# One mask product for both query tiles, the geodesic difference in halves, clips of two banks, and a new instruction order

## What is computed

```python
cos = jnp.einsum('bhsd,bhtd->bhst', q, k)            # q, k of length 1
g_dist = jnp.arccos(jnp.clip(cos, -1.0 + EPS, 1.0 - EPS))
attn_score = (1.0 + g_dist) ** (-3.2)
```

## Time and profile before

| | |
|---|---|
| median of 3 runs | 2499.11 us |
| the profiled execution's own time | 2502.13 us |
| its span, first to last instruction | 2500.8 us |
| TensorE busy with products | 1993.4 us, 10866 instructions |
| VectorE busy | 1930.0 us, 3005 |
| ScalarE busy | 1833.5 us, 2759 |
| GpSimd busy | 525.0 us, 206 |
| mean granted TensorE clock | 0.842 of full speed |

### The profile page before, as it was taken

How to read it: one execution, slowest core, us unless ns; L and a number is a source line. 1 busy time by engine, 2 the same in 40 slices (tenths; PEclk the granted TensorE clock), 3 DMA queues, 4 the chain that set the end, 5 groups by cost and what they waited for, 6 DMA issues and landing times.

```text
span 2500.8 us, 32678 instructions
## 1 busy us (share of the span) xinstructions
PE 1993.4 (80%) x10866; PEld 1328.3 (53%) x10866; DVE 1930.0 (77%) x3005; ACT 1833.5 (73%) x2759; POOL 525.0 (21%) x206
## 2 busy tenths in 40 slices
PE   4777778888678878878787888878787878888867
PEld 2544546775345555655465555655455555655645
DVE  5788895545997889699867889699968889674554
ACT  3436868697669677887777787887678786978883
POOL 2413121022112121302212121302112211221220
PEclk8787878999887888888787989888687989776778
DMA  7631112432211110111001110111001010000000
GB/s 250 222 98 56 51 34 67 131 116 85 83 42 53 46 35 18 40 35 55 22 13 48 39 48 13 40 46 53 13 31 39 32 53 1 1 1 5 1 1 5
DMA packets 67527, 126.29 MB, mean 51 GB/s; under 512 B 8836, under 2 KB 40132, under 8 KB 67236
## 3 DMA queue, kind: packets, MB, share of 16 engines
q1 hardware_dynamic: 61808, 113.19, 13.9%
q0 software_dynamic: 2816, 7.21, 0.8%
q10 hardware_dynamic: 2740, 3.80, 0.4%
HBM read 111.33 MB, written 12.85 MB: 50 GB/s over the span
## 4 chain that ended last, share of the span: by engine, by line
PE 31%; DVE 30%; ACT 18%; issue 16%; DMA 2%; SPq 1%; POOL 1%; DVEq 0%; ACTq 0%; POOLq 0%
PE ps L763 6%; DVE hB L1434 5%; PE ps L984 4%; PE ps L942 4%; DVE hB L1428 3%; DVE hB L1440 2%; PE ps L1068 2%; ACT arena L1255 2%; ACT arena L1331 2%; PE ps L1043 2%; DVE arena L1506 2%; DVE n_c L1513 2%; ACT L758 2%; PE ps L1103 2%; DVE lss L1568 2%
## 5 line engine op out<-in xcount | busy, mean ns | idle before, releaser
L1726 POOL TENSOR_TENSOR arena<-arena 128x2048 f32<-128x2048 f32 x64 | 297.5, 4649 | 1188.9 <-ACT arena L1257 1188.8
L763 PE MATMUL ps<-w_ident,arena 128*128 128x128 f32 x1647 | 301.1, 319 | 123.6 <-ACT arena L1331 43.7
L942 PE MATMUL ps<-hB,w_ident 128*128 128x512 f32 x512 | 303.4, 725 | 75.3 <-DVE hB L1440 75.2
L763 PEld LDWEIGHTS ps<-w_ident,arena 128*128 128x128 f32 x1647 | 227.7, 166 | 234.1 <-issue 139.1
L1434 DVE TENSOR_TENSOR_SCAN hB<-dA,hB 128x1024 f32<-128x1024 f32 x128 | 324.6, 2539 | 9.1 <-ACT dA L1219 8.8
L1730 POOL TENSOR_TENSOR arena<-arena,rb 128x1024 f32<-128x1024 f32 x64 | 151.9, 2374 | 574.6 <-DVE rb L1566 574.6
L1219 ACT ACTIVATE dA<-dtv,w_A_log 128x510 f32<-128x510 f32 x256 | 168.8, 718 | 109.6 <-DVE hB L1434 108.6
L1043 PE MATMUL ps<-w_l_wqkv,arena 128*128 128x512 f32 x384 | 212.5, 677 | 33.7 <-DVE lss L1568 15.5
L1506 DVE TENSOR_SCALAR arena<-ps 128x512 f32<-128x512 f32 x256 | 163.8, 681 | 63.6 <-PE ps L984 62.8
L1331 ACT ACTIVATE arena<-ps,nmx 128x128 f32<-128x128 f32 (+1 forms) x512 | 158.9, 397 | 65.5 <-DVE nmx L1588 64.8
L942 PEld LDWEIGHTS ps<-hB,w_ident 128*128 128x128 f32 x512 | 106.3, 229 | 181.9 <-issue 116.2
(11 more groups left out here) (198 smaller groups left out, 4216.3 us busy)
## 6 DMA issues: line engine op xcount, KB each, us to landing
BC<-bc_d SPq DMA_DIRECT2D x128, 512.0 KB, 3.7
BC<-in_experts SPq DMA_DIRECT2D x31, 514.0 KB, 3.3
arena<-in_experts SPq DMA_DIRECT2D x15, 514.0 KB, 3.6
arena<-in_x SPq DMA_DIRECT2D x8, 256.0 KB, 5.8
xnT_d<-arena SPq DMA_DIRECT2D x8, 256.0 KB, 3.7
hB<-xnT_d SPq DMA_DIRECT2D x8, 256.0 KB, 2.6
x<-in_x SPq DMA_DIRECT2D x8, 256.0 KB, 2.9
out<-go SPq DMA_DIRECT2D x8, 256.0 KB, 2.3
```

Source lines behind the costliest of these rows:

```text
L763: return t.transpose(out_, in_, ident[0:k, 0:k])
L942: e = t.matmul(lb(), ident, hB[k % 2][:, j], start=q == 0 and j == 0, stop=q == NQ - 1 and j == NG - 1)
L1726: g.tensor_tensor(la[m % 2], la[m % 2], cl, ALU.subtract).then_inc(g_sub, 1)
```

## The change

- **Mask.** A `score` unit writes the mask of a head for both query tiles with one product of 320 columns (256 products in all instead of 512), and both mask products now stand ahead of all score products.
- **Difference.** `g_sub` becomes two GpSimd instructions of 128 by 1024, each for two heads. The clips of a half wait only for the same half of the block before; tanh and `f_tr`, whose tile shares memory with `cl`, wait for both halves.
- **Clips.** The two clips of a `g_score` unit become one over both banks (128 instructions of 128 by 1024). For this `choose` gives `g_score` two neighbouring banks.
- **Order.** `LATER`, `SWITCH` and the four constants have new values, `STREAM` adds an offset for some pairs of a kind of block (Mamba, geodesic, window layers), and three durations in `STAGES` differ (`g_score` VectorE 1.3 to 1.2, `g_sub` 4.6 to 2.4 a half, `score` TensorE 1.7 to 1.4). Every unit may change its place in the lists.

```diff
-SWITCH = 67.0
+SWITCH = 79.0
...
+STREAM = {("g", 5): -52, ("l", 0): -2, ("l", 2): -4, ("l", 6): 1, ("l", 7): -2, ("m", 1): -1, ("m", 2): -5, ("m", 4): -1,
+          ("m", 6): 17, ("m", 7): -10}
...
+def stream(unit):
+    u, n, b, k = unit
+    if u in [x for x, _ in LAYER]:
+        return "l", n // LAY
+    return ("-" if u == "m_weights" else u[0][0]), n
...
-        want[what] = time + LATER.get(what[0], 0.0)
+        want[what] = time + LATER.get(what[0], 0.0) + STREAM.get(stream(what), 0.0)
...
-EARLY, FIRST, SECOND, PERIOD = 49.0, 120.0, 105.0, 239.0
+EARLY, FIRST, SECOND, PERIOD = 120.0, 130.0, 80.0, 210.0
...
-        if unit[0] != "score":
+        if unit[0] not in ("score", "g_score"):
             return sorted(idle[0:count]) if len(idle) >= count else None
         pairs = [[z, z + 1] for z in range(7) if z in idle and z + 1 in idle]
...
+        def two_banks(unit):
+            z0, z1 = plan["banks"][unit]
+            return ps[:, z0:z1 + 1:z1 - z0]
...
+                    for z in range(2):
+                        t.matmul(lb(z)[:, 0:SC], ident_b[:], mask_b[:], start=True, stop=False)
                     for qt in range(2):
-                        for z in range(2):
-                            cols = slice(P, SC) if qt else slice(0, P)
-                            t.matmul(lb(z)[:, cols], ident_b[:], mask_b[:, cols], start=True, stop=False)
                         for z in range(2):
...
-                    a.wait_ge(g_sub, m + 1)
+                    a.wait_ge(g_sub, 2 * (m + 1))
...
                     if m:
-                        v.wait_ge(g_sub, m)
+                        v.wait_ge(g_sub, 2 * (m - 1) + k % 2 + 1)
                     v.wait_ge(p_gs, 2 * m + k % 2 + 1)
-                    for z in range(2):
-                        v.tensor_scalar(cl[:, 2 * (k % 2) + z], lb(z), -1.0 + 1e-7, 1.0 - 1e-7, ALU.max, ALU.min).then_inc(v_gs, 1)
+                    v.tensor_scalar(cl[:, 2 * (k % 2):2 * (k % 2) + 2], two_banks(unit), -1.0 + 1e-7, 1.0 - 1e-7,
+                                    ALU.max, ALU.min).then_inc(v_gs, 1)
...
-                    m = BLOCKS * i + HB * b + k
+                    m = BLOCKS * i + HB * b + k // 2
+                    half = slice(2 * (k % 2), 2 * (k % 2) + 2)
                     g.wait_ge(a_ln, m + 1)
-                    g.tensor_tensor(la[m % 2], la[m % 2], cl, ALU.subtract).then_inc(g_sub, 1)
+                    g.tensor_tensor(la[m % 2][:, half], la[m % 2][:, half], cl[:, half], ALU.subtract).then_inc(g_sub, 1)
```

More of the change, by code:

```diff
@@ L81 @@
          "norm": "ln", "score": "ln", "ln": "ln", "m_in": "silu", "g_tan": "tan", "gelu": "gelu"}
-SWITCH = 67.0
[L84 to L89, removed]
+SWITCH = 79.0
+LATER = {"down": 15, "f_ln": 16, "f_tr": -17, "f_xn": -23, "f_yg": 129, "g_av": 1, "g_ev": 1, "g_hd": -89, "g_ln": 25,
+         "g_norm": 84, "g_out": -34, "g_pow": 23, "g_qkv": -33, "g_score": -56, "g_sq": -5, "g_sub": -26, "g_tan": 9,
+         "gelu": -28, "heads": 2, "hid": 15, "l_weights": -74, "ln": 39, "ln2": 26, "lnT": -79, "m_B": 95, "m_C": 56,
+         "m_bx": 2, "m_dt": 15, "m_du": 28, "m_ex": 55, "m_fin": 128, "m_hc": 149, "m_in": -22, "m_load": 33, "m_out": -15,
+         "m_scan": -5, "m_weights": -52, "m_xp": 33, "norm": -2, "on": 21, "out": 47, "pv": 13, "qkv": -4, "qn": -8,
+         "score": -1, "up": 4, "x_load": 22, "zeros": 46}
+STREAM = {("g", 5): -52, ("l", 0): -2, ("l", 2): -4, ("l", 6): 1, ("l", 7): -2, ("m", 1): -1, ("m", 2): -5, ("m", 4): -1,
+          ("m", 6): 17, ("m", 7): -10}
 LOADED = [15.0, 24.0]
@@ L184, in all_units @@
         unit(start - 20, ("f_xn", i), ("f_ln", i))
-        unit(start - 20, ("f_tr", i), ("f_xn", i), *[("g_sub", i - 1, 1, HB - 1) for z in range(1) if i])
+        unit(start - 20, ("f_tr", i), ("f_xn", i), *[("g_sub", i - 1, 1, 2 * HB - 2 + z) for z in range(2) if i])
         for tt in range(TT):
@@ L987, in tensor_program @@
                     for z in range(2):
-                        read_by(unit, v_gs, HB * m + 2 * (k % 2) + z + 1, z)
+                        read_by(unit, v_gs, 2 * m + k % 2 + 1, z)
                 elif u == "g_av":
@@ L1067, in tensor_program @@
                             o_, j0 = (lb(z)[:, P:SC], WIN) if qt else (lb(z)[:, 0:P], 0)
-                            e = t.matmul(o_, q_, kT[head_rows(z), k, b * L + j0:b * L + (L if qt else P)], start=False, stop=True)
+                            e = t.matmul(o_, q_, kT[head_rows(z), k, b * L + j0:b * L + (L if qt else P)], start=False, stop=qt == 1)
                     e.then_inc(p_sc[b], 1)
@@ L1584, in vector_program @@
                     hs = slice(2 * (k % 2), 2 * (k % 2) + 2)
-                    z0, z1 = plan["banks"][unit]
-                    both = ps[:, z0:z1 + 1:z1 - z0]
+                    both = two_banks(unit)
                     v.tensor_reduce(nmx[b][:, 0, hs], both[:, :, 0:P], AX.X, ALU.max, negate=True)
```

23 lines of the change are left out of this document (13 added, 10 removed).

## The result

The changed kernel takes 2490.48 us against 2498.81 (medians of 20 runs each); the ratio is 0.9965, 95% interval 0.995 to 0.998. So it is 0.35% faster, 8.7 us, where 30 were forecast. It lies inside the stated range (2418 to 2520) and on the side that was forecast, at under a third of the size. The profiled execution took 2490.14, its span is 2488.9, against 2502.13 and 2500.8 before: 12 us less.

What follows compares the result with a forecast made beforehand. Bound: VectorE and TensorE handing work over in the middle, a chain's order in the tail. Terms 4 + 3.7 + 16 = 24, kept at 19, plus 11 for order: 30 off 2502.1, 2472, median 3 lower: 2469 us (2418 to 2520).

Steps and rivals of the forecast that it cites:

- What bounds the kernel: VectorE and TensorE handing work over in the middle, chain order in the tail; 128 us of VectorE stretched beside GpSimd differences.
- The mask: TensorE's mask products: 256 fewer save 13.5 us (0 to 22), by 31% of the chain 4 us of kernel.
- 0.6 us for all: By the skill's gap rule, 256 products fewer save 0.6 us of TensorE and nothing on the chain.
- The clips: VectorE's two clips merged into one: 12 us of busy time saved (0 to 22), 3.7 us of kernel.
- The halves: Blocked VectorE instructions get in between GpSimd's two halves: 20 us of VectorE, 0.8 on the chain, 16 us.
- Four fifths: Share kept of the 24 us from mask, clips and halves, as other engines are close: 19 us.
- The order: Planner's new order of all units: a gain of 11 us, the widest term, leaning to the tail.
- 19 + 11: Whole kernel: 19 us from mask, clips and halves plus 11 from the new order, 30 us less.
- Stalls only move: Rival: GpSimd's second half wins or the next two-input VectorE instruction pays; 2493 us, chance 0.15.
- bank pairs: Slower rival: TensorE's queue waits for two neighbouring banks ahead of geodesic scores; 2541 us, chance 0.09.
- More collisions, or another poor order: Slower rival: more GpSimd differences meet two-input VectorE instructions (2534 us if all 64), or a poor order; chance 0.12.
- Wrong if the busy time falls by 30 and the span doesn't follow: Sign against the prediction: VectorE's busy time falls by 30 us and the kernel's span doesn't follow.

Runs made afterwards that it cites:

- e4: Kernel before, in its own order, with the GpSimd difference cut to 8 columns (its result left out): ratio 0.9565 to the kernel before.
- e5: Kernel before, in its own order, with the one mask product and the difference in halves: ratio 0.9877 to the kernel before.
- e12: Kernel before, in its own order, with the one mask product and the difference in four parts of 512 columns: ratio 0.9708 to the kernel before.
- e1: Kernel before, in its own order, with only the one mask product of 320 columns: ratio 0.9942 to the kernel before.
- e7: Changed kernel, in its new order, with two clips of 512 a unit again: ratio 0.9937 to the kernel before.
- e3: Changed kernel's order and banks with the old instructions (four mask products, two clips, whole difference): ratio 1.0121 to the kernel before.
- e2: Kernel before, in its own order, with only the GpSimd difference in two halves: ratio 0.9898 to the kernel before.
- e11: Changed kernel with two clips a unit and any two free banks for the geodesic scores, planned anew: ratio 0.9945 to the kernel before.
- e9: Kernel before, old instructions and due times, with neighbouring banks required for the geodesic scores, planned anew: ratio 1.0178 to the kernel before.
- e10: Changed kernel, in its new order, with each half of the difference cut to 8 columns (result left out): ratio 0.9532 to the kernel before.
- e15b: Changed kernel, in its new order, with each half of the difference as two instructions of 512 columns: ratio 0.9785 to the kernel before.
- e13b: Kernel before with `PERIOD` 240 instead of 239, planned anew: ratio 1.0036 to the kernel before.
- e14b: Kernel before with `EARLY` 50 instead of 49, planned anew: ratio 1.0133 to the kernel before.

## Why the prediction was right and wrong

- *What bounds the kernel.* Right in the reading that mattered. The loss inside VectorE's busy time was real and on the path: e4 gives 0.88 us of kernel for one us of it, where 0.8 was read off the chain. That rate is no constant: from halves to quarters the kernel gained 42 us for 17 of stretch (e5, e12).
- *The mask.* The saving was too small, the share was not. The mask products' own part came as told at full clock (0.10 us a unit for 0.09), but the score products behind them became quicker by 0.20, which the prediction put at nothing without a reason. TensorE saved 37 us by the page, outside the bounds of 0 to 22, where 13.5 was taken. Of that 14 us arrive (e1), 0.39, and the chain's 0.31 lies in the interval. The prediction read "some 50 ns a product beyond its columns"; it is rather a cost where mask and score products follow each other. The Trainium skill, TensorE: Matmul & The Clock Gate, Back-to-back issue gap, gives N/2.4 + 2.5 ns from one product to the next for a product by itself, and says that this is too little at small N in a stream with weight loads. Where two mask products follow each other at full clock the trace is near it: 56, 93 and 135 ns for 128, 192 and 320 columns, from start to start, where the rule has 56, 82.5 and 136. It doesn't give the change from one kind to the other: from the last score product of 128 columns to a mask product it is 204 ns (median, before), to the next score product 105 (e1). The two kinds differ in type (bf16 and float32) and in the rows that they use (128 and 64); which of these costs the time wasn't tested. The "0.6 us for all" by that rule is far from the 37.
- *The clips.* VectorE's saving was 8 us for 12; on the kernel nothing that shows (e7), for 3.7.
- *The halves.* Mechanism and size right: 22 us of stretch for 20. On the kernel 25 in the old and 18 in the new order, for 16.
- *Four fifths.* 0.77 measured (e5), with intervals that would allow much else.
- *The order.* The step that failed, as the prediction put it: "I take a gain of 11, near to no change with a lean to the tail". No row stood behind the 11. It was a loss: 30 us with the old instructions (e3), 15 with mask and halves (e7 against e5), 22 if the merged clips are counted to it (0.9965 - 0.9877). The tail became longer by 26 to 32 us where it was to give, though with more work in it. The mistake was to treat the order of before as one of many alike and a new one as drawn around it. All four others that were run on its instructions were slower, and so were all three on the instructions of mask and halves, which fits an order that was already a chosen one.
- *The sum.* 31 from mask and halves, and 22 lost through the order with the clips: 9. The 22 is what is left over, so that this comes to the 8.7 measured proves nothing. Taken the other way, the order costs 30 (e3) and the instructions bring 39 in it. Under 19 + 11 in the forecast lie two errors that pull apart, a gain too small by at least 12 and an order wrong by at least 33. That the time still fell on the forecast side of no change is in part luck.
- *The rivals.* "Stalls only move" is refuted by e2. Of "bank pairs" the waits came in part (57.0 us of idle time before the geodesic scores for 31.2), but not their price: e11 without the rule and e7 with it take the same time, though e9 looked otherwise. "More collisions, or another poor order" came true in its second half: with the old instructions the stretched sum is smaller in the new order (161 for 170), so it was not a matter of more collisions.
- *What it was to be known by.* The mask products (21.4 less), the clip, the longest scan and the shorter period (266.4) came as told. A half of 2.37 came in the median (2359 ns), not in the mean (2758, with its wait inside). The sign of TensorE waiting ahead of the geodesic scores showed too, without a price. "Wrong if the busy time falls by 30 and the span doesn't follow": that is the case. VectorE's fell by 28, TensorE's by 26, and the kernel by 8.7.

**Still open.** Why the other orders are slower: e10 points to the place of the collisions with GpSimd, e15b and e12 point away from it. In the five profiles of the same instructions TensorE is busy for longer in the slower kernels: 1993 us before, then 2005 (e13b), 2025 (e3), 2033 (e14b) and 2017 (e9), at granted clocks of 0.842, 0.838, 0.830, 0.832 and 0.833. Busy time by clock is 1678 to 1692 in all five, and 1680 in the kernel without the difference, so the busy time differs because the clock does. That kernel's page has:

```profile
PE 1935.4 (81%) x10866; PEld 1296.4 (54%) x10866; DVE 1806.8 (76%) x3005; ACT 1830.6 (77%) x2759; POOL 248.1 (10%) x206
```

The same products take 58 us less than before where VectorE isn't held up (clock 0.868 for 0.842). The clock thus goes roughly with the gains and the losses. Which comes first, the clock or the gaps between products, no run here separates, and it may have a part in each exchange rate above.

## What to carry to other kernels

Look for instructions whose longest duration is a multiple of their median: the loss is in busy time and no view of waits names it. Cut the instruction of the idle engine beside which the others are held up, and go on cutting until the fixed cost of a piece shows; here the change stopped at two parts and eight were best. When an instruction is taken out from between others, count what its neighbours gain too: here that was twice its own saving. Where a kernel's order comes out of a search, price the instruction changes in the frozen order first: planning anew is a change of its own, with a spread (here 0.4 to 1.8% in four orders, all slower) that must be measured and not counted as zero.

## What was not expected of the hardware

- A VectorE instruction that is held up by a GpSimd instruction is served before the next GpSimd instruction (the longest scan 4.44 us with halves, 6.55 without), and GpSimd then waits inside its own (a pair of halves 6.64 us for 4.67 undisturbed).
- Small instructions pay the full price: a VectorE product of 128 by 512 that usually takes 0.7 us took 2.77 behind a half, and one of 32 columns took 4.49 beside a whole difference.
- GpSimd's parts cost little more for being small: in the median 4.53 us whole, 2.36 a half, 1.27 a quarter and 0.73 an eighth, so eight take 5.8 us. With the waits inside them the means are 1553 ns a quarter and 988 ns an eighth.
- Score products between mask products take 0.20 us a unit longer at full clock than the same ones behind each other (0.95 and 0.75 us).
- Taking away 123 us of VectorE's held-up time took 109 us off the kernel, although VectorE is busy for only 77% of it.
